# Transposes of 64 tokens in two row groups and two banks, in a stack of four cross-attention layers

## What is computed

```python
def grouped(x, cond, wq, wk, wv, wo, norm_w):         # layers 0 and 2
    xn = rmsnorm(x, norm_w)
    q = (xn @ wq).reshape(B, T, 4, 4, 32)
    k = (cond @ wk).reshape(B, S, 4, 32); v = (cond @ wv).reshape(B, S, 4, 32)
    attn = softmax(einsum('btgrd,bsgd->bgrts', q, k) / sqrt(32))
    return x + einsum('bgrts,bsgd->btgrd', attn, v).reshape(B, T, 512) @ wo

def masked(x, cond, mask_A, mask_B, Wq, Wk, Wv, Wo, bo, idx_A, idx_B):   # layers 1 and 3
    q, k, v = heads(x @ Wq), heads(cond @ Wk), heads(cond @ Wv)          # 16 heads of 64
    logits = q @ k.T * 64 ** -0.5 + col_bias          # col_bias: -20 * (1 - mask) at idx columns
    return x + (softmax(logits) @ v) @ Wo + bo
```

## Time and profile before

| | us |
|---|---|
| median of 3 runs (lowest to highest) | 1507.51 (1506.37 to 1511.48) |
| the profiled execution: its time | 1509.95 |
| the profiled execution: its span, first to last instruction | 1508.2 |
| TensorE busy in the span | 1487.8 (99%) |
| VectorE, GpSimd, ScalarE busy | 989.6, 912.7, 744.5 |
| mean granted TensorE clock | 0.998 |

### The profile page before, as it was taken

How to read it: one execution, slowest core, us unless ns; L and a number is a source line. 1 busy time by engine, 2 the same in 40 slices (tenths; PEclk the granted TensorE clock), 3 DMA queues, 4 the chain that set the end, 5 groups by cost and what they waited for, 6 DMA issues and landing times.

```text
span 1508.2 us, 23315 instructions
## 1 busy us (share of the span) xinstructions
PE 1487.8 (99%) x8480; PEld 1232.5 (82%) x8480; DVE 989.6 (66%) x1644; ACT 744.5 (49%) x1317; POOL 912.7 (61%) x825
## 2 busy tenths in 40 slices
PE   7998999999999999999999999999999999999998
PEld 7987887888778887888788877888788877887787
DVE  5676757765776657665776667565766577666764
ACT  4566576335733564346633573346533663357321
POOL 0074467557765587567756686468756775568541
PEclk9999999999999999999999999999999999999999
DMA  9999562122312231132212232143113231222101
GB/s 323 327 405 409 199 232 91 42 79 84 126 52 69 98 119 50 44 126 83 79 46 76 92 112 64 34 136 119 43 43 103 81 101 53 65 99 91 57 1 56
DMA packets 101649, 170.12 MB, mean 113 GB/s; under 512 B 17056, under 2 KB 51360, under 8 KB 95520
## 3 DMA queue, kind: packets, MB, share of 16 engines
q1 hardware_dynamic: 97552, 151.06, 30.3%
q10 hardware_dynamic: 3824, 17.04, 2.8%
q0 software_dynamic: 160, 0.53, 0.1%
HBM read 116.95 MB, written 51.65 MB: 112 GB/s over the span
## 4 chain that ended last, share of the span: by engine, by line
PE 87%; POOL 4%; DVE 3%; ACT 2%; SPq 1%; DMA 1%; issue 1%; ACTq 0%; DVEq 0%
PE OB L375 16%; PE OB L376 15%; PE OB L377 15%; PE SB L375 10%; PE SB L377 9%; PE SB L376 9%; POOL xhl L1344 4%; PE TB L507 3%; PE MX L507 3%; PE TB L543 1%; PE SB L484 1%; DMA s_fm<-prob 1%; PE OB L430 1%; PE OB L427 1%; ACT xhl L851 1%
## 5 line engine op out<-in xcount | busy, mean ns | idle before, releaser
L1315 POOL TENSOR_TENSOR prob<-prob,small 128x512 f32<-128x512 f32 x256 | 278.7, 1091 | 255.3 <-DVE small L1115 255.0
L816 ACT ACTIVATE prob<-prob 128x512 f32<-128x512 f32 x128 | 80.8, 632 | 274.2 <-DVE prob L1102 271.6
L1093 DVE SCALAR_TENSOR_TENSOR prob<-SB,aux 128x512 f32<-128x512 f32 x128 | 88.0, 688 | 182.4 <-PE SB L377 181.8
L1309 POOL TENSOR_TENSOR prob<-prob,small 128x512 f32<-128x512 f32 x128 | 136.2, 1064 | 117.3 <-DVE small L1087 117.0
L375 PE MATMUL SB<-foldM,xhl 128*128 128x512 f32 x512 | 203.9, 398 | 1.6 <-issue 0.3
L375 PE MATMUL OB<-pT,foldN 128*128 128x512 f32 x512 | 205.0, 400 | 0.0
L376 PE MATMUL OB<-pT,foldN 128*128 128x512 f32 x512 | 199.8, 390 | 0.0
L377 PE MATMUL SB<-foldM,xhl 128*128 128x512 f32 x512 | 199.7, 390 | 0.0
L377 PE MATMUL OB<-pT,foldN 128*128 128x512 f32 x512 | 199.7, 390 | 0.0
L376 PE MATMUL SB<-foldM,xhl 128*128 128x512 f32 x512 | 199.4, 389 | 0.0
L1087 DVE TENSOR_REDUCE small<-prob 128x8 f32<-128x512 f32 x128 | 87.1, 680 | 93.0 <-ACT prob L826 91.6
(11 more groups left out here) (140 smaller groups left out, 3851.4 us busy)
## 6 DMA issues: line engine op xcount, KB each, us to landing
prob<-in_wkvM_dram SPq DMA_DIRECT2D x32, 512.0 KB, 8.4
ring<-s_fm SPq DMA_DIRECT2D x64, 256.0 KB, 5.5
ring<-s_fn SPq DMA_DIRECT2D x128, 128.0 KB, 2.6
out_dram<-x ACTq DMA_DIRECT2D x15, 1024.0 KB, 3.9
s_fm<-prob SPq DMA_DIRECT2D x16, 512.0 KB, 8.4
wraw<-in_wqG_dram SPq DMA_DIRECT2D x8, 1024.0 KB, 6.8
s_fn<-x SPq DMA_DIRECT2D x16, 512.0 KB, 5.8
ring<-in_xT_dram SPq DMA_DIRECT2D x32, 256.0 KB, 3.2
```

The costliest lines, as they stand in the source:

```text
L816: act.activation(own, own, ACT.Exp).then_inc(S["exped"], 1)
L1093: dve.scalar_tensor_tensor(out=own, in0=bank, scalar=M_SCALE, in1=row, op0=ALU.mult, op1=ALU.add).then_inc(S["biased"], 1)
L1309: pool.tensor_tensor(own, own, hmax[u % 2].unsqueeze(2).broadcast_to([P, HH, KEYS]), ALU.subtract).then_inc(S["evac"], 1)
L1315: pool.tensor_tensor(own, own, rsum[u % 2].unsqueeze(2).broadcast_to([P, HH, KEYS]), ALU.mult).then_inc(S["normed"], 1)
```

## The change

- A transpose now takes 64 tokens (64 partitions of `prob`, a row group) and 128 keys. The lower 64 tokens of each group of 128 go to TB and the upper 64 to MX, alternating. `transposes(it, ph, p, ...)` handles the two key chunks 2p and 2p + 1 together: 16 transposes, and both banks are signalled at its end.
- `pt_hi` and `pt_lo` still copy 128 x 512 each, now half of the tokens of two chunks, in runs of 64 elements. A product waits for both halves of its pair.
- `pT` holds four chunks; the semaphore `prodd` and its waits are gone.
- In phase 3 chunks 0 and 1 are both transposed in `masked_grouped`, and `pt_hi`, `pt_lo` of both come before `xb_hi` and `xnew`.
- `sqsum` is gone: squares are summed in place in `xsq[:, 0]`, new ones go to `xsq[:, 1]`. `cst` has its own memory and `spare` lies in `pF`.

The diff, cut to its core:

```diff
         xsq = sb("xsq", [P, 2, BLK])
-        sqsum = sb("sqsum", [P, BLK])
+        cst = sb("cst", [P, 64])
         prob = [sb(f"prob{b}", [P, TT, HK]) for b in range(2)]
-        pT = sb("pT", [P, 2, 2, BLK], F32R)
+        pT = sb("pT", [P, 4, 2, BLK], F32R)
         pF = sb("pF", [P, 4, BLK])
         ring = sb("ring", [P, 4, BLK])
-        spare = sb("spare", [P, BLK])
         aux = sb("aux", [P, AUX])
...
             return kG4[32 * r:32 * r + 32, :, :, KEYS * r:KEYS * (r + 1)].bitcast(F32), src
+
+        def pt_part(ph, t, part):
+
+            p, r = t // 2, t % 2
+            if ph in (1, 2):
+                two = pF[:, 2 * p % 4:2 * p % 4 + 2, :]
+            else:
+                two = pT[:, 2 * p % 4:2 * p % 4 + 2, part, :]
+            return two.rearrange("p c (tt r n) -> p r c tt n", r=2, n=P // 2)[:, r]
+
+        def t_out(t):
+
+            return t_bank(t)[:, :].rearrange("p (c tt n) -> p c tt n", c=2, n=P // 2)
         def fold_part(i, part):
...
                 for tt in range(TT):
-                    last = pe.matmul(SB[1][:, tt:tt + 1], sqsum[:, tt * P:(tt + 1) * P], ones, start=True, stop=True)
+                    last = pe.matmul(SB[1][:, tt:tt + 1], xsq[:, 0, tt * P:(tt + 1) * P], ones, start=True, stop=True)
                 last.then_inc(S["qchunk"], 1)
-            def transposes(it, ph, t, first, tail=False):
+            def transposes(it, ph, p, first, tail=False):
+
                 k = 4 * it + ph
                 pr = prob[(ph - 1) % 2]
-                pe.wait_ge(S["normed"], 8 * (k - 1) + 4 * (t // 4) + 4)
-                if first and ph == 1 and t < 2:
-                    pe.wait_ge(S["ev_d" if t else "ev_a"], 2 * MASKED)
+                pe.wait_ge(S["normed"], 8 * (k - 1) + 4 * (p // 2) + 4)
+                if first and ph == 1 and p == 0:
+                    pe.wait_ge(S["ev_a"], 2 * MASKED)
+                    pe.wait_ge(S["ev_d"], 2 * MASKED)
                 elif ph == 0:
-                    pe.wait_ge(S["pt_lo"], 16 * it - 8 + max(t - 1, 0))
-                elif ph == 3 and t > 1:
-                    pe.wait_ge(S["pt_lo"], 16 * it + t - 1)
-                elif ph == 1 and t < 2:
+                    pe.wait_ge(S["pt_lo"], 16 * it - 8 + 2 * p)
+                elif ph == 3 and p > 0:
+                    pe.wait_ge(S["pt_lo"], 16 * it + 2 * p)
+                elif ph == 1 and p == 0:
                     pe.wait_ge(S["pt_lo"], 16 * it)
-                elif t < 2:
-                    pe.wait_ge(S["ot_lo"], 4 * (2 * it + ph - 2) + 3 + t)
-                elif t in (4, 5):
-                    pe.wait_ge(S["ot_lo"], 4 * (2 * it + ph - 1) + t - 3)
+                elif p == 0:
+                    pe.wait_ge(S["ot_lo"], 4 * (2 * it + ph - 1))
+                elif p == 2:
+                    pe.wait_ge(S["ot_lo"], 4 * (2 * it + ph - 1) + 2)
                 else:
-                    pe.wait_ge(S["pt_hi"], 8 * (k - 1) + t - 1)
-                out = t_bank(ph, t)
-                for tt in range(TT):
-                    last = pe.transpose(out[:, tt * P:(tt + 1) * P], pr[:, tt, t * P:(t + 1) * P], ident[:, :])
-                last.then_inc(S["trans"], 1)
+                    pe.wait_ge(S["pt_hi"], 8 * (k - 1) + 2 * p)
+                for c in range(2):
+                    for tt in range(TT):
+                        for r in range(2):
+                            rows = slice(64 * r, 64 * r + 64)
+                            keys = slice((2 * p + c) * P, (2 * p + c + 1) * P)
+                            cut = slice(c * 256 + tt * 64, c * 256 + tt * 64 + 64)
+                            last = pe.transpose(t_bank(r)[:, cut], pr[rows, tt, keys], ident[rows, rows])
+                            if c == 1 and tt == TT - 1:
+                                last.then_inc(S["trans"], 1)
             def open_out(it, ph, c, tail=False):
...
             def product(it, ph, t, first, tail=False):
-                pe.wait_ge(S["pt_lo"], 16 * it - 8 * (ph == 0) + t + 1)
+                pe.wait_ge(S["pt_lo"], 16 * it - 8 * (ph == 0) + 2 * (t // 2) + 2)
                 if ph == 3:
                     last = three(OB[c][:, :], foldN[:, 0, t, c * P:(c + 1) * P], foldN[:, 1, t, c * P:(c + 1) * P],
-                                 pT[:, t % 2, 0, :], pT[:, t % 2, 1, :], t == 0, t == KC - 1)
+                                 pT[:, t % 4, 0, :], pT[:, t % 4, 1, :], t == 0, t == KC - 1)
                     if t == KC - 1:
                         last.then_inc(S["outd"], 1)
-                if t in (1, 3, 5):
-                    last.then_inc(S["prodd"], 1)
             def mixing(it, ph, m):
...
             def masked_masked(it, first):
-                transposes(it, 3, 1, first)
                 for s in range(1, STEPS):
                     if s % 2 == 0:
-                        transposes(it, 3, s, first)
-                        transposes(it, 3, s + 1, first)
+                        transposes(it, 3, s // 2, first)
                     product(it, 3, s - 1, first)
                     transposes(ITS, 0, 0, False, True)
-                    transposes(ITS, 0, 1, False, True)
                 scores(it, 3, STEPS - 1, first)
             def body(it, first):
...
                 if c >= 2:
-                    act.wait_ge(S["sq_added"], 3 * a + 1)
+                    act.wait_ge(S["sq_added"], 3 * a + c - 1)
+                elif c == 1 and not (first and ph == 0):
+                    act.wait_ge(S["sq_added"], 3 * a)
                 elif not (first and ph == 0):
-                    act.wait_ge(S["sq_added"], 3 * a - 1 + c)
-                act.activation(xsq[:, c % 2, :], ring[:, c, :], ACT.Square).then_inc(S["x_sq"], 1)
+                    act.wait_ge(S["qchunk"], 4 * a)
+                act.activation(xsq[:, min(c, 1), :], ring[:, c, :], ACT.Square).then_inc(S["x_sq"], 1)
             def ws_hi(it, i):
...
             def pt_hi(it, ph, t):
                 act.wait_ge(S["trans"], 8 * (4 * it + ph - 1) + t + 1)
-                if ph in (0, 3) and t in (3, 5, 7):
-                    act.wait_ge(S["prodd"], 3 * (2 * it - (ph == 0)) + t // 2)
-                to = pT[:, t % 2, 0, :] if ph in (0, 3) else pF[:, t % 4, :]
-                act.activation(to, t_bank(ph, t)[:, :], ACT.Copy).then_inc(S["pt_hi"], 1)
+                act.activation(pt_part(ph, t, 0), t_out(t), ACT.Copy).then_inc(S["pt_hi"], 1)
             def ot_hi(a, j):
                 act.wait_ge(S["mixed"], 2 * a + j // 2 + 1)
-                act.activation(oT[:, 0, j % 2, :], t_bank(1, j)[:, :], ACT.Copy).then_inc(S["ot_hi"], 1)
+                act.activation(oT[:, 0, j % 2, :], t_bank(j)[:, :], ACT.Copy).then_inc(S["ot_hi"], 1)
             def part_hi(it, i, first):
...
                 pt_hi(it, 3, 0)
+                pt_hi(it, 3, 1)
                 exp(it, 2, STEPS - 1)
                 act.wait_ge(S["outd"], 16 * it + 8)
-                pt_hi(it, 3, 1)
                 for s in range(1, STEPS):
-                    if s >= 2:
+                    if s % 2 == 0:
                         pt_hi(it, 3, s)
+                        pt_hi(it, 3, s + 1)
                     if s <= 4:
...
                 pt_lo(it, 3, 0)
+                pt_lo(it, 3, 1)
                 xnew(it, 2)
                 xb_lo(it, 2)
-                pt_lo(it, 3, 1)
                 sums(it, 2, STEPS - 2, first)
                 for s in range(1, STEPS):
-                    if s >= 2:
+                    if s % 2 == 0:
                         pt_lo(it, 3, s)
+                        pt_lo(it, 3, s + 1)
                     evac(it, 3, s - 1, first)
...
                 pool.wait_ge(S["x_sq"], 4 * a + c + 1)
-                if c == 1:
-                    if not (first and ph == 0):
-                        pool.wait_ge(S["qchunk"], 4 * a)
-                    pool.tensor_tensor(sqsum[:, :], xsq[:, 0, :], xsq[:, 1, :], ALU.add).then_inc(S["sq_added"], 1)
-                else:
+                if c > 1:
                     pool.wait_ge(S["sq_added"], 3 * a + c - 1)
-                    pool.tensor_tensor(sqsum[:, :], sqsum[:, :], xsq[:, c % 2, :], ALU.add).then_inc(S["sq_added"], 1)
+                pool.tensor_tensor(xsq[:, 0, :], xsq[:, 0, :], xsq[:, 1, :], ALU.add).then_inc(S["sq_added"], 1)
             def part_lo(it, i):
```

More of the change, by code:

```diff
@@ L117, in bass_cross_attention_stack @@
                  "ld_kg ld_x0 ld_x1 ld_aux stored0 stored1 scores copied biased maxed evac shifted "
-                 "exped hsummed summed normed trans prodd pt_hi pt_lo mixed ot_hi ot_lo outd xnew xb_hi xb_lo_p xb_lo_d "
+                 "exped hsummed summed normed trans pt_hi pt_lo mixed ot_hi ot_lo outd xnew xb_hi xb_lo_p xb_lo_d "
                  "qchunk qd q_hi q_lo x_hi x_lo x_sq rmsd sq_added powd invd fold_hi fa_lo fb_lo").split()
@@ L143, in bass_cross_attention_stack @@
         kG4 = kG[:, :, :].rearrange("p s (j n) -> p s j n", j=KVH)
-        cst = sqsum[:, 0:64]
+        spare = pF[:, 2, :]
```

(29 more changed lines are left out.)

10 lines of the change are left out of this document (4 added, 6 removed).

## The result

| | before | after |
|---|---|---|
| median, us (lowest to highest; runs) | 1507.37 (1506.37 to 1511.48; 6 runs) | 1515.85 (1514.95 to 1516.64; 6 runs) |
| ratio, 95% interval | | 1.0051 (1.0039 to 1.0064) |
| the profiled execution: time, span | 1509.95, 1508.2 | 1514.95, 1513.1 |
| mean granted TensorE clock | 0.998 | 0.999 |

The change makes the kernel slower by 8.5 us by the medians; the ratio, which is one of means, gives 7.7, with 5.9 to 9.6 by its interval. The likeliest case was right in direction and too small.

The account below looks back on a forecast made before the run. TensorE was taken as the bound, except at few places per iteration where the chain leaves it. Terms -4.8 + 4.8 + 1.5 + 1.9 - 0.4 gave +3.0 us, so 1510.5 us; range 1499 to 1522 for 8 in 10.

Parts of the forecast that it names:

- The likeliest case: Whole kernel: small group savings outweighed by waits at three places, +3.0 us in sum, 1510.5 us; chance 0.70.
- The group: Sixteen half transposes between full matmuls take 0.824 us against 0.87, edges included; 104 groups save 0.046 each, -4.8 us.
- Rival A: Transposes: the row groups' loads do not overlap, or 64-row loads take as long as ordinary ones; +48 us, 1556; chance 0.12.
- rival B: Transposes: no emptying between transposes and matmuls, and a pair period of 0.0545 us; -41 us, 1467; chance 0.06.
- The three places: transposes(it, 3, 0), (it, 2, 1) and (it, 2, 0), 8 of each, lose +4.8, +1.5 and +1.9 us.
- rival C: The three places do not grow, as queues read as full take up the shift; 1501.6 us; chance 0.12.
- the first: transposes(it, 3, 0): a second pt_lo on VectorE ahead of xnew delays the chain by 0.6 us, 8 times, +4.8 us.
- the second: transposes(it, 2, 1): TB is signalled only at the group's end, 0.19 us later, 8 times, +1.5 us.
- the third: transposes(it, 2, 0): all sixteen wait until MX is free, 0.24 us more, 8 times, +1.9 us.
- Edits at about nothing: Four-chunk pT, evacuation in 64-element runs, squares in place and memory moves: nothing, except -0.4 us for a late bank.
- the late bank: One bank in grouped_masked, 0.06 us late, is freed by the four-chunk pT, 7 times, -0.4 us.
- The squares: Square sum in xsq: the fourth square waits for the second addition, with no margin; costed at 0.

Follow-up runs that it names:

- 3: The changed kernel with every group of sixteen half transposes done twice into the same places; 1569.90 us.
- 4: The kernel before the change with every chunk's four whole transposes done twice; 1612.66 us.
- Experiment 7: The changed kernel with phase 3's chunks 0 and 1 as whole 128-token transposes and x between their low parts; 1510.82 us, ratio to before 1.0020.
- Experiment 1: The changed kernel with whole transposes of 128 tokens again, everything else of the change kept; 1519.93 us, ratio to before 1.0076.
- experiment 8: The changed kernel with weight parts behind the pair's in grouped_masked and transposes, copies and other queue entries of phases 1 to 3 re-ordered; 1505.16 us, ratio 0.9975.
- Experiment 2: The changed kernel with part_hi and part_lo of weight chunks 1 and 3 moved behind the pair's pt_hi and pt_lo in grouped_masked; 1513.45 us, ratio 1.0035.
- 6: The kernel before with squares summed in place and nothing else of the change; 1508.63 against 1509.05 us, ratio 1.0006.
- experiment 5: The changed kernel with the eight half transposes of the lower tokens first, then the eight of the upper ones; 1543.54 us.

## Why the prediction came out as it did

**The bound.** That TensorE's time is the kernel's time, up to a few places per iteration, held: doubling transposes (3, 4) cost what they cost TensorE, less the waits that they filled.

**The group.** Right in mechanism, a little off in size. The edges are there at 0.09 us each way with loads that aren't made ahead, and the period is 0.0625, not 0.060: 0.344 + 8 x 0.0625 = 0.844, measured 0.84. The saving is 0.036 by the shifts in place of 0.046, so -3.7 in place of -4.8. Rival A (loads that don't overlap) fell with the first pair of rows, and rival B with the edges. By the Trainium skill ("TensorE: Matmul & The Clock Gate", section LDWEIGHTS) 128 columns should have set a pace of 107 ns; loads and streams follow each other here every 62.5 ns. Its "TensorEngine Tiling (Array Packing)" is borne out on both sides: in experiments 3 and 4 the added work of a group costs 0.50 against 0.87, 1.75 times less (section Theoretical Speedup promises up to 2), and the drain at a change of mode (section Key Properties), for which the page gives no time, takes most of that back in a group of only sixteen.

**The three places.** All grew, so rival C fell, by 0.70, 0.17 and 0.28 where 0.6, 0.19 and 0.24 were given: +9.2 in place of +8.2. Experiment 7 shows the first by removing it. Experiment 1 shows the second (it goes when TB is signalled by itself) and bears out the third (0.43 for a whole group of whole transposes, as worked out beforehand); experiment 8 removed the wait for `foldN`, but together with other moves.

**The step that failed** is in "Edits at about nothing": `pT` and the product's wait for both chunks in `grouped_masked`, costed at 0 because "two copies and two subtractions need 0.3 + 0.5 + 0.6 + 0.7 = 2.1 us" under 2.7 us of matmuls, and ScalarE is 49% busy. The four durations are right; the queue is missing. ScalarE began on the banks 1.2 us after the group, behind an `exp` and a weight's high part, and VectorE had the weight's low part (0.9 us) ahead. From the group's end to the second `pt_lo`'s end it took 1346.5 - 1342.75 = 3.75 us and not 2.1. (The cover was under-counted as well: 3.7 us with the scores, which is why the wait is only 0.25.) A mean busy share says nothing of what stands in a queue at one moment. The text named the consequence ("TensorE would wait for pT") and gave it no price and no chance. It cost +3.6 us. The -0.4 booked beside it for the late bank did come (-0.5). Experiment 2 took the whole of the 3.6 away by order alone.

Together: the sum moves from +3.0 to +8.6, by 3.6 for the failed step, 1.1 for the groups, 1.0 for the three places and -0.1 for the bank. The squares (6) were rightly nothing. That the time still fell inside the range is partly luck: the range was widened upwards for a doubling of the three waits, and most of the excess came from a place booked at nothing.

**Expectations that missed.** Those of 3 and 4 forgot that added work fills waits; that of 5 held the order for all or nothing, while TensorE lets the second row group start five halves late; that of 8 moved a wait within a queue that was full.

## What to carry to other kernels

Before booking a new wait as covered, write out the queue of each engine that feeds it, at that place, from the trace: start of the first free moment, what stands ahead, end of the last; a sum of the durations alone is a lower bound. Joining two signals into one (two banks, two chunks) makes the first result as late as the second, and where an engine's queue behind it is full, re-ordering that queue doesn't pay; only taking work out of it does. A faster form of a short group must first pay for its two edges: here 0.37 us saved inside the group left 0.04.

## What the hardware showed that I hadn't expected

- A transpose of f32 with a load of 64 rows by 128 columns and a stream of 64 keeps its row group busy for 0.0625 us, above the 0.0545 that half of a 128-column stream would take; alone or beside the other row group makes no difference (experiment 5). That the load sets this pace is likely and not shown: no run changed the load without the stream.
- Whole f32 transposes take 0.109 us each (experiment 4), though their loads have followed each other after 0.06: their loads don't set that pace.
- With one row group's instructions all ahead of the other's, the second started 0.30 us, five halves, after the first (experiment 5). Why five is open.
